# Choosing 128 places twice with one one-hot, and two moved steps, in a mixture-of-experts / attention kernel

## The reference

```python
x = x + 0.5 * ffn(layernorm(x), gate_w, w_gate, w_up, w_down)
x = x + attn(layernorm(x), Wq, bq, Wk, bk, Wv, bv, Wo, bo)
x = x + 0.5 * ffn(layernorm(x), ...)          # the same weights again
```

```python
affinity = softmax(x @ gate_w.T)              # (batch, token, expert)
gating, idx = top_k(affinity by expert, 256)  # 256 of 1024 tokens, per batch and expert
h = silu(x[idx] @ w_gate.T) * (x[idx] @ w_up.T)     # inner width 512
out[idx] += gating * (h @ w_down.T)
```

## Time and profile before

| | |
|---|---|
| time, median of 3 runs | 1262.96 us (1261.88 to 1264.34) |
| time of the profiled execution | 1251.99 us |
| its span | 1249.9 us |
| mean granted clock of TensorE | 0.962 |
| busy: PE, DVE, ACT, POOL | 1083.5, 981.6, 777.4, 562.9 us |
| passes 0 to 15 | about 78 to 320 us |
| attention, groups 0 to 15 | about 320 to 1006 us |
| passes 16 to 31 | about 1006 to 1226 us |
| last adds to DRAM | to the end |

### The profile page before, as it was taken

One profiled execution on the slowest core, in us unless ns is written; L12 is line 12 of the kernel. 1 busy time (PEld: TensorE's weight loads), 2 busy tenths in 40 slices (PEclk: granted clock), 3 DMA queues, 4 the chain that ended last, 5 costly groups with the idle time before them and its releaser, 6 DMA issues.

```text
span 1249.9 us, 25039 instructions
## 1 busy us (share of the span) xinstructions
PE 1083.5 (87%) x9344; PEld 461.4 (37%) x9344; DVE 981.6 (79%) x1962; ACT 777.4 (62%) x1475; POOL 562.9 (45%) x573
## 2 busy tenths in 40 slices
PE   3169897899489899999989999899999879899994
PEld 3036565566232122222222222222222246556663
DVE  3675965565888899999989999799997674875641
ACT  2035231433258899999979999799999936232220
POOL 3035878465646331000011466335621035568886
PEclk9999999899778899999999999899999988999998
DMA  8014455347803131211121121111220125345453
GB/s 264 24 31 106 88 117 125 60 92 181 215 34 95 29 91 41 57 42 47 25 51 40 42 60 33 47 41 40 63 66 12 34 58 122 77 88 100 110 118 30
DMA packets 92704, 93.71 MB, mean 75 GB/s; under 512 B 14572, under 2 KB 69868, under 8 KB 92552
## 3 DMA queue, kind: packets, MB, share of 16 engines
q1 hardware_dynamic: 70056, 75.33, 21.5%
q0 software_dynamic: 22528, 16.79, 9.5%
HBM read 63.84 MB, written 30.06 MB: 75 GB/s over the span
## 4 chain that ended last, share of the span: by engine, by line
PE 47%; DVE 24%; issue 13%; ACT 11%; POOL 2%; SPq 1%; DMA 1%; DVEq 0%; POOLq 0%; ACTq 0%
DVE mx L1751 16%; ACT Pt L1073 9%; PE pS L1241 8%; PE pA L1252 8%; PE pO L1376 7%; PE pS L1397 4%; PE pO L1242 4%; PE pS L1242 4%; PE pA L1312 3%; DVE ge L1467 2%; PE pA L1221 2%; PE pS L1160 1%; DVE onehot L1545 1%; PE pA L1132 1%; ACT U L1064 1%
## 5 line engine op out<-in xcount | busy, mean ns | idle before, releaser
L1751 DVE TENSOR_REDUCE mx<-pA 128x2 f32<-128x1024 f32 x512 | 585.9, 1215 | 20.2 <-PE pA L1312 19.9
L1073 ACT ACTIVATE Pt<-pS 128x512 f32<-128x512 f32 x1024 | 556.2, 596 | 41.5 <-PE pS L1397 36.2
L1376 PE MATMUL pO<-Pt,Vst 128*16 128x256 f32 x4096 | 323.1, 388 | 12.8 <-ACT U L1064 12.8
L588 POOL DMA_INDIRECT xg<-zd,idx x128 | 125.8, 983 | 197.8 <-DVE idx L1560 129.3
L972 ACT ACTIVATE Pt<-pS 128x512 f32<-128x512 f32 x128 | 76.2, 596 | 221.3 <-PE pS L1241 221.3
L1312 PE MATMUL pA<-Kst,Qst 48*128 48x512 bf16 x704 | 139.9, 394 | 20.9 <-DVE mx L1751 19.7
L1241 PE MATMUL pS<-Pt,wg 128*128 128x512 f32 x256 | 141.7, 636 | 17.6 <-issue 11.0
L1376 PEld LDWEIGHTS pO<-Pt,Vst 128*16 128x16 f32 x4096 | 68.1, 94 | 208.2 <-issue 111.8
L1397 PE MATMUL pS<-Qst,Kst 51*128 51x512 bf16 x704 | 139.1, 391 | 6.7 <-ACT Pt L1073 3.8
L659 POOL TENSOR_TENSOR mparts<-mx,onesm 128x32 bf16<-128x32 f32 x16 | 4.0, 252 | 278.9 <-DVE mx L1756 218.2
L1252 PEld LDWEIGHTS pA<-wd,Pt 128*128 128x128 f32 x960 | 114.7, 194 | 17.6 <-issue 17.1
(11 more groups left out here) (212 smaller groups left out, 1130.5 us busy)
## 6 DMA issues: line engine op xcount, KB each, us to landing
wg<-w_gate_dram SPq DMA_DIRECT2D x32, 256.0 KB, 2.7
wu<-w_up_dram SPq DMA_DIRECT2D x32, 256.0 KB, 3.2
wd<-w_down_dram SPq DMA_DIRECT2D x32, 256.0 KB, 3.9
qk<-parts SPq DMA_DIRECT2D x64, 96.0 KB, 2.4
Kst<-qk SPq DMA_DIRECT2D x132, 32.0 KB
zd<-Z SPq DMA_DIRECT2D x8, 512.0 KB
vp<-pair SPq DMA_DIRECT2D x4, 1024.0 KB, 5.1
Vst<-vp SPq DMA_DIRECT2D x16, 256.0 KB
```

Of the source, the lines that this page charges most:

```text
L588: pool.indirect_dma_start(xg[p][:, k, :], None, zd[j // E % 2], bass.IndirectOffsetOnAxis(idx[j % 6][:, k:k + 1], 0)).then_inc(s_gath[p], 16)
L1073: S.activation(Pt[:, s % 4, j, r * 512:(r + 1) * 512], pS[:, bank_of(k, 4 * s + 2 * j + r), :], ACT.Exp, scale=SCALE).then_inc(s_exp, 1)
L1376: last = M.matmul(pO[32 * h:32 * h + 16, cols], Vst[k][:, s % 8, h, :], Pt[:, s % 4, h // 2, (h % 2) * 512 + 256 * a:(h % 2) * 512 + 256 * ...
L1751: V.reduce_max(mx2[:, k, 2 * j:2 * j + 2, c, half], pA[ring[q, a] % 2][:, :, :], AX.X).then_inc(s_Ar, 1)
```

## The change

Four edits. (1) The one-hots get 128 places in place of 256. Tokens whose place is above 128 are marked in `upper`; 128 is taken off their place (`place_in`), and the five values stand in two sets of columns, `columns`: in the first set those of tokens with a place up to 128, in the second those of the others, zero elsewhere. `by_slot` builds it, on POOL for halves 0 and 2, on DVE for 1 and 3. `compact` then has 16 products with 10 moving columns in place of 32 with 5. (2) `room` becomes a buffer of its own, and the one-hots its first half. (3) The output projections of batches 0 and 1 move from behind pieces 24 and 27 of groups 7 and 11 to behind pieces 1 and 4 of groups 8 and 12. (4) `load_weights(10)` stands ahead of the loads of X.

```diff
-    behind = {(7, 24): ("p", 0, 0), (7, 27): ("p", 0, 1), (11, 24): ("p", 1, 0), (11, 27): ("p", 1, 1)}
+    behind = {(8, 1): ("p", 0, 0), (8, 4): ("p", 0, 1), (12, 1): ("p", 1, 0), (12, 4): ("p", 1, 1)}
...
-        slotT = [sb(f"slotT{h}", [P, HT, E], F32) for h in range(2)]
+        slotT = sb("slotT", [P, HT, E], F32)
+        upper = [sb(f"upper{h}", [P, HT, E], BF16) for h in range(2)]
+        place_in = [sb(f"place_in{h}", [P, HT, E], F32) for h in range(2)]
+        columns = [sb(f"columns{h}", [P, HT, E, SH, 5], BF16) for h in range(2)]
...
-        onehot = sb("onehot", [P, HB, CH, CAP], BF16)
+        room = sb("room", [P, 2, N], F32)
+        onehot = room[:, 0, :].bitcast(BF16).rearrange("p (b c s) -> p b c s", b=HB, c=CH)
...
-            for j in range(2, 10):
+            for j in range(2, 11):
                 load_weights(j)
             for b in range(2):
                 sp.wait_ge(s_scat[b], 256)
                 load_x(b, x1_in)
-            for j in range(10, 15):
+            for j in range(11, 15):
                 load_weights(j)
...
+            def by_slot(hh):            # POOL; the same on DVE with V in place of GP
+                v = vals[hh % 2][:, :, :, :]
+                high = upper[hh % 2][:, :, :].unsqueeze(3).to_broadcast([P, HT, E, 5])
+                to = columns[hh % 2]
+                pool.wait_ge(s_vals, 6 * hh + 6)
+                pool.wait_ge(s_upper, hh + 1)
+                GP.tensor_tensor(to[:, :, :, 1, :], v, high, ALU.mult).then_inc(s_above, 1)
+                pool.wait_ge(s_above, hh + 1)
+                GP.tensor_tensor(to[:, :, :, 0, :], v, to[:, :, :, 1, :], ALU.subtract).then_inc(s_columns, 1)
...
             gains(0)
+            by_slot(0)                  # POOL, ahead of gather(0)
             gather(0)
...
+            by_slot(2)                  # POOL, behind the attention's loop
             gather(RUN)
...
                 if j % E == 0:
-                    pe.wait_ge(s_vals, 6 * (j // E + 1))
+                    pe.wait_ge(s_columns, j // E + 1)
                 for b in range(HB):
                     pe.wait_ge(s_onehot, 2 * j + b + 1)
-                    for s in range(SH):
-                        for c in range(CH):
-                            last = M.matmul(pI[:, (b * SH + s) * 5:(b * SH + s + 1) * 5],
-                                            onehot[:, b, c, s * P:(s + 1) * P], vals[j // E % 2][:, c * HB + b, j % E, :],
-                                            start=(c == 0), stop=(c == CH - 1))
+                    for c in range(CH):
+                        last = M.matmul(pI[:, b * SH * 5:(b + 1) * SH * 5], onehot[:, b, c, :],
+                                        columns[j // E % 2][:, c * HB + b, j % E, :, :].rearrange("p s f -> p (s f)"),
+                                        start=(c == 0), stop=(c == CH - 1))
...
-                    V.tensor_scalar(slotT[hh % 2][:, :, :].rearrange("p t e -> p (t e)"), bank[:, 0:P], -1.0, None,
-                                    ALU.add).then_inc(signal_read(key), 1)
+                    V.tensor_scalar(flat(upper[hh % 2]), bank[:, 0:P], float(P + 1), None, ALU.is_ge).then_inc(s_upper, 1)
+                    V.tensor_scalar(flat(slotT), bank[:, 0:P], -1.0, None, ALU.add).then_inc(signal_read(key), 1)
+                    dve.wait_ge(s_upper, hh + 1)
                     dve.wait_ge(*was_read(key))
+                    link(V.scalar_tensor_tensor(flat(place_in[hh % 2]), flat(upper[hh % 2]), -float(P), flat(slotT),
+                                                ALU.mult, ALU.add))
...
-                    last = V.tensor_scalar(onehot[:, b, c, :], slots[:, :], slotT[j // E % 2][:, c * HB + b, e:e + 1], None,
+                    last = V.tensor_scalar(onehot[:, b, c, :], slots[:, 0:P], place_in[j // E % 2][:, c * HB + b, e:e + 1], None,
                                            ALU.is_equal)
...
                 if (it, k) == (6, 0):
                     all_onehots(8)
+                    by_slot(1)
...
                 if (it, k) == (21, 4):
                     all_onehots(24)
+                    by_slot(3)
```

More of the change, by code:

```diff
@@ L211, in program @@
         num, den = scr[:, 0:2, :], scr[:, 2:4, :]
-        room = onehot[:, :, :, :].rearrange("p b c s -> p (b c s)").bitcast(F32).rearrange("p (i n) -> p i n", i=2)
         pairs = {4: (scr[:, 0, :], scr[:, 2, :]), 5: (scr[:, 1, :], scr[:, 3, :]), 6: (room[:, 0, :], room[:, 1, :]),
@@ L267, in program @@
         s_onehot = sem("onehot")
+        s_upper = sem("upper")
+        s_above = sem("above")
+        s_columns = sem("columns")
         s_comp = sem("comp")
@@ L1520, in front @@
                 else:
[L1521 to L1522 removed]
+                    flat = lambda a: a[:, :, :].rearrange("p t e -> p (t e)")
+                    V.tensor_scalar(flat(upper[hh % 2]), bank[:, 0:P], float(P + 1), None, ALU.is_ge).then_inc(s_upper, 1)
+                    V.tensor_scalar(flat(slotT), bank[:, 0:P], -1.0, None, ALU.add).then_inc(signal_read(key), 1)
+                    dve.wait_ge(s_upper, hh + 1)
                     dve.wait_ge(*was_read(key))
+                    link(V.scalar_tensor_tensor(flat(place_in[hh % 2]), flat(upper[hh % 2]), -float(P), flat(slotT),
+                                                ALU.mult, ALU.add))
             def affinities(hh):
@@ L1540, in affinities, with by_slot @@
                 last.then_inc(s_affc, 1)
+            def by_slot(hh):
+                v = vals[hh % 2][:, :, :, :]
+                high = upper[hh % 2][:, :, :].unsqueeze(3).to_broadcast([P, HT, E, 5])
+                to = columns[hh % 2]
+                dve.wait_ge(s_vals, 6 * hh + 6)
+                V.tensor_tensor(to[:, :, :, 1, :], v, high, ALU.mult).then_inc(s_above, 1)
+                dve.wait_ge(s_above, hh + 1)
+                V.tensor_tensor(to[:, :, :, 0, :], v, to[:, :, :, 1, :], ALU.subtract).then_inc(s_columns, 1)
             def onehots(j, quarter):
```

## The result

| | before | after | ratio |
|---|---|---|---|
| median | 1262.42 us (1260.32 to 1264.34) | 1243.72 us (1240.42 to 1245.18) | 0.9849 [0.9821, 0.9876] |
| the same again, another chip | 1252.64 us (1246.66 to 1255.49) | 1228.20 us (1226.84 to 1230.91) | 0.9817 [0.979, 0.9844] |
| and a third | 1251.55 us (1246.85 to 1256.71) | 1233.62 us (1229.57 to 1236.32) | 0.9848 [0.9818, 0.9878] |

In brackets behind a ratio stands its 95% interval. The change saves 18.7, 24.4 and 17.9 us where 23.4 were forecast; 1243.7 lies in the range of 1232 to 1248 around 1239.6. What the chips differ in, the ratio takes out. The three intervals overlap, so the runs don't show that the saving differs from chip to chip. The executions of one kernel do differ among each other, and the profiles show where: mostly in stages in which TensorE's granted clock falls behind a wait.

A forecast was written before the change was run, and what follows sets the result against it. Bounds taken: DVE in attention and search passes, SyncE's order at pass 10, POOL's queue at the end. Sum 7.6 + 10.4 + 4.5 + 2.4 - 1.0 - 0.5 = 23.4 us off 1262.96: 1239.6 us, range 1232 to 1248 (own range 1235 to 1243).

The forecast's parts named there:

- Rival A: Pass 10: weights share DMA engines and land 7 us behind `down`; 4 us gained, not 7.6; 1243 us; chance 9%.
- rival B: Attention: loads of groups 8 and 12 replace the stall; gain 10.4 falls to 5 or 6; 1245 us; chance 9%.
- Rival C: Start and pass 6: building `columns` is the new wait; 4 and 2.5 us lost; 1244 to 1245 us; chance 10%.
- rival E: `compact` on PE: ten moving columns cost twice five, so 4.5 us are missing; 1244 us; chance 3%.
- Weights of pass 10, 7.6: Pass 10: weights issued earlier; pass starts 5.5 us sooner, 2.2 more from TensorE's clock; 7.6 us gained, between 4 and 8.6.
- Output projections, 10.4: Attention groups 7, 8, 11, 12: later projections no longer wait for `num`; 5.5 + 6.3 - 1.4 = 10.4 us gained.
- `compact`, 4.5: PE's compactions: 0.39 us saved each, counted where PE is the bound with no wait behind; 4.5 us gained.
- rival D: Pass starts: longer PE waits lower TensorE's clock, 2.2 us each; 26 lost against 23.4 won; 1265.6 us; chance 3%.
- One-hots, 2.4: DVE's one-hots in the chain: halved width saves 34 ns of 202 each; 2.4 us gained (0 to 4.8).
- The start, -1.0: Before pass 0: compaction waits for POOL's `by_slot(0)` beside DVE's one-hots; 1.0 us lost (gain 0.3 to loss 2.5).
- `by_slot(1)`, -0.5: Pass 6: two DVE products of about 0.83 us each delay PE; 0.5 us lost (0 to 1.0).
- POOL's queue in the second half: From `gather(23)` to the end: POOL's unbroken gathers and scatters decide the end, 136 us as before; `compact` saves nothing there.

The follow-up runs named there:

- products against the waits: After, plus matrix products with overwritten results, five ahead of pass 2 and seven in pass 11: 1231.81 us, ratio 0.9843 to before.
- last version: After, plus split `by_slot`, third weight buffers, pass 2's weights before Z stores, seven overwritten products in pass 11, group loads before inverse sums: 1225.89 us, ratio 0.9794.

## Why the prediction was right, point by point

The two moves, 18.0 of the 23.4 us, were right in mechanism and nearly in size. The rest, and the agreement of the totals, owe much to chance. The absolute time, 1243.7, lies just above the forecast's own range of 1235 to 1243 and where rivals A, B, C and E had put it (1243 to 1245); B and C did come true in part. And it rests on 11.0 us between profiled and timed executions that were no constant: after's first profiled execution took 1245.18 us and not the 1228.6 of the sum, 1.5 above its median. The saving is what can be compared, 18.7, 24.4 and 17.9 us. Of the prediction's own signs three failed: DVE was busy less than 95% of both windows, PE stood for the loads of group 8, which it had named as a sign that the forecast is wrong, and POOL's last stretch had holes.

- **Weights of pass 10, 7.6.** Right in mechanism, somewhat small: 9.1 us by undoing it, 9.4 in the stage. The wait came out at 1.20, 0.55 and 2.43 us in the three profiles of after where about 1 was expected, each time with the first pair behind it at 1.10. In the second profile of before the stall itself was 7.65 us, and 8.07 with the weights put back, not 6.24; that is where the rest comes from. Rival A did not come.
- **Output projections, 10.4.** 10.4 by undoing them and 9.8 in the stages when done alone; in after 7.7, because of rival B at the first site: the margin of 1.1 us that the prediction called narrow was used up, PE waited 1.5 us for Vst of group 8, and the site is 78.3 us long where the second is 76.2. That rival was priced at 5 in all, and it is 2.1, at one of the two sites and not in every variant.
- **`compact`, 4.5.** 16 products take 0.38 us (0.39 forecast), rival E is out. What failed in the sum is that the saving counts in passes 0 and 2, and in rival D that "my waits stay below 1.2". What the passes 0 and 1 save ends in a wait for pass 2's weights, whose landing the prediction never looked up. That wait was there already (1.40 us in before) and grew to 2.6 to 2.8: by 0.5 us because PE is ready sooner after the stores of Z, and by 0.7 to 0.9 because the weights land later after them. The clock did the rest: pass 2 takes 20.7, 25.9 and 27.2 us against 18.2, 19.9 and (moves alone) 19.7. This is rival D, in one pass and not in fifteen, worth 1 to 9 us; whether the 1 becomes 9 is chance, as far as these runs tell. In the second half the waits ahead of passes reach 1.88 us, above the 1.2 too, and the pair behind still takes 1.10.
- **One-hots, 2.4.** 32 ns saved per instruction (34 forecast), 16 in a row 2.70 us (2.69). They and the compaction together give 0.6 to 1.0 us in passes 3 to 5, 0.8 in 12 to 14, 1.0 behind the last group (not in the first profile) and 1.9 in 20 and 21.
- **The start, -1.0.** It is 1.8 to 1.9 us, because DVE, not POOL, loses; the second start, ahead of pass 16, has the same rows (1.27 and 3.70 us), hidden by the last group as forecast.
- **`by_slot(1)`, -0.5.** Its two products are 0.87 and 0.81 us (0.83 forecast), the pass is 1.1 us longer.
- **POOL's queue in the second half.** The length of this stretch hardly moves (141.7, 142.5 before; 143.3 to 145.6 after), and the waits ahead of the passes took the compaction's saving, as said, and 1 to 4 us more. "Unbroken" was wrong: all three profiles of after have holes in it, the longest 3.34, 1.04 and 1.89 us (before none and one of 0.96). That PE, now waiting up to 1.88 us for weights ahead of a pass, falls behind POOL there fits this, but no run tests it. The longest:

```profile
1221.82 1.55 POOL L617 DMA_INDIRECT out_dram<-Pt,idxo  x1 [3.34 <-issue]
```

So the layout of the one-hots, forecast at 5.4 us net (4.5 + 2.4 - 1.0 - 0.5), brought 2.0 beside the moves, within the uncertainty of the comparison; the moves brought 16.0 alone, and 10.4 and 9.1 when each was undone. The parts of the layout don't add up to these 2.0: undoing the compaction cost 2.6 to 6.5 us and widening the one-hots 5.1 to 9.0, and the start and pass 6 cost 3.0, which would leave 4.7 at the least. So what the layout is worth is known only to some us. The total came near because a gain sized too small (pass 10) stands against losses sized too small (the start, pass 2, the loads of group 8). Rival C was real at both places, at 3.0 us in place of 6.5, where 1.5 were charged.

Open: why the clock falls in one execution and not in the next behind the same wait. In pass 11 PE stood for 3.0 us ahead of the same products in after's second profile, and for 2.96 in the one with the projections back. In the former the clock fell to 0.50 and the pass took 19.6 us, in the latter it stayed at 1.00 and the pass took 16.7, as in after's third profile behind 2.92. And the stop of all engines near 990 in after's first profile (3.48 us, put down to no engine or known queue) was seen once.

## What to carry to other kernels

Before an engine is made quicker, look up the wait that stands next on it: a saving that ends in a wait is lost, and a wait made longer can cost more than the saving, since the matrix engine may come out of it at half its clock. Read for each awaited transfer what stands ahead of it in its queue, and what that waits for; here the weights of pass 2 stood behind stores that waited for ScalarE, and a third buffer did nothing for them until their place changed. When an instruction on POOL moves, look at which DVE instruction it will meet. Stages without a fall of the clock repeat between executions to some 0.1 us, others and the totals only to several us, so measure small edits by the stages of at least two profiles, and count only what repeats.

## What the runs showed of the hardware

- A DVE instruction with its data in SBUF stood until POOL's product on SBUF was over, and POOL lost nothing: `place_in` took 1.27 us in place of 0.29 beside a product of 1.29, the first one-hot 1.25 in place of 0.24 beside one of 1.31, the instruction that closes a group 2.05 and 2.11 in place of 0.19 beside products of 2.36 and 2.35; they ended 0.04 to 0.15 us behind it. POOL's product of 560 columns took 1.15 us beside DVE and 1.16 without.
- DVE's pieces, which read PSUM, kept their 1.21 us beside such a product of 2.37 us (after's third profile, 630.72).
- POOL can be the one that loses: 128 columns took it 1.05 us among short instructions of DVE, 0.46 beside a piece that reads PSUM.
- Behind one and the same wait the granted clock stays at 1.00 or falls to 0.50, for 3 to 17 us: pass 2 with a wait of 1.20 to 1.40 us took 18.2 to 19.9 us (four profiles, two with a fall), with one of 2.57 to 2.82 20.7 to 27.2 (eight profiles, all with a fall).
- The clock also fell with no wait ahead, in the last 0.7 us of 32 products of 8 columns that kept PE busy for 3.7 and 3.9 us (products against the waits, last version).
